# Retention with its fp32 operands kept as pairs of 16-bit parts, and small work moved between VectorE, ScalarE and GpSimd

## The chip, the cores and the metric

The kernel runs on one core of one Trainium2 chip. The metric is the device time of one execution in microseconds, and the time of a kernel is the median over its runs. Five engines work side by side, each through its own row of instructions in order: TensorE (PE; its weight loads are shown as PEld), VectorE (DVE), ScalarE (ACT), GpSimd (POOL) and SyncE (SP), which starts transfers. They wait for each other by semaphores alone.

## The reference

The program is a two-layer decoder on x of 2 x 1024 x 256 with a context of 2 x 154 x 192: a table-based attention, a cross attention and a mixture of experts in the first layer, then multi-scale retention, a headed cross attention and a signed feed-forward in the second. Every sublayer is pre-norm with a residual. The change touches retention alone, which has 16 heads with keys of 16 and values of 32:

```
x  = layernorm(x)                                  # rows of 256
q, k, v, g = x@q_w+q_b, (x@k_w+k_b)*16**-0.5, x@v_w+v_b, x@g_w+g_b
qr, kr = theta_shift(q, sin, cos), theta_shift(k, sin, cos)
mask   = where(tril, exp(diff*decay), 0);  mask /= sqrt(mask.sum(-1))
qk     = einsum('bhmd,bhnd->bhmn', qr, kr) * mask
qk     = qk / clip(abs(qk.sum(-1)), 1)
out    = einsum('bhmn,bhnd->bhmd', qk, v)
out    = (out - out.mean(-1)) / sqrt(out.var(-1) + 1e-5)    # per head, 32 wide
y      = (silu(g) * out) @ o_w + o_b               # and x += y
```

## The kernel before

All 2048 rows of x stay in SBUF as 16 tiles `x[:, t]` of 128 rows by 256. `retention` (L2608) works through the tiles in a software pipeline that is written out by hand: every engine runs `for s in STEPS` with s from -2 to 18, and in step s it works on tile s for the scores and the state, s+1 for values and turned queries and keys, s+2 for the projection and rotation of queries and keys, s-1 for the products and gates, s-2 for the gated output and s-3 for the residual. The rows of x for tile s+4 are turned and those of tile s+5 are normalised (`x_center`). The order of the calls in each loop is the order of the instructions on that engine. Nothing else orders the work but the semaphores.

Eight tiles make one batch (TB = 8). Inside a tile all 128 x 128 scores are formed; what lies in earlier tiles of the batch comes through a state `us` of (16 keys + 16 idle rows) x 33 per head, which `state` updates on VectorE from `delta`'s product and multiplies by a decay, and which is spread over four head rows into `u` for the next tile. So the first tile of each batch (t = 0 and 8) has no product with the state.

One step in the order of the data, with the lines of before:

- PE `qk` (L2948, 6 matmuls of 512 columns, 16-bit parts) projects into the bank `psq`. VectorE `rotate` turns it there in four operations (L2779, 2780, 2781, 2785), the last of which writes the fp32 tile `rot` (16 elements a head, and 16 zeros) and frees psq (`rot_done`).
- PE `turn_qk` transposes the queries, ScalarE copies them to `qkT` (L2859), then the same for the keys. Both copies are 512 wide and use the one bank `ptr`.
- PE `score` (L2922) multiplies keys and queries in fp32, two halves of 8 matmuls with K=32; each half fills `pss`. ScalarE `high` (L2852) takes a 16-bit copy of 1024 columns, VectorE `low` (L2726) the 16-bit rest, and GpSimd `mask` (L2686) zeroes the future in both parts, two operations a half.
- PE `values` (L2948) projects into the bank `psv`. ScalarE copies it twice, as 16-bit (L2867, `vhi_done`) and as fp32 `v32` (L2868, `v_done`); VectorE takes the difference of the two copies (`values_low`, L2734).
- PE `weigh` fills `pso`: for each of four groups of heads one fp32 product with the state `u` of 132 columns (L2937) and twelve 16-bit ones of 33 columns (L2941). PE `delta` (L3022) forms keys times values in fp32, 16 matmuls of 33 columns in four column groups.
- ScalarE `squares` copies pso (L2843) and squares it (L2845). VectorE `centre` has four operations: two on the row factors (L2762, L2763, 16 elements each), the sum of the squares (L2765), and the variance (L2767). GpSimd `power` raises it to -0.5 (L2705).
- PE `gates` projects the gates into the same bank `psv`; ahead of it stands a wait for v_done, since the values of tile s+1 must have left it. ScalarE `silu` (L2879), then VectorE `gate` in two operations (L2749, and L2752 after pow_done) gives `z`; it is turned, split in two 16-bit parts, multiplied by the output weights (L2982) and added to x.
- GpSimd `expand` (L2695) spreads the state into `u`, one operation of 528 elements.

Every fp32 matmul shows as two records on PE. `own.link` or `L` marks an instruction and lets the next one on the same engine wait for its end. A bank such as psv is one PSUM bank, and the trace names it `r_psv`.

Of the kernel before, what the change touches and what calls it, by code (L numbers as in the profile page):

```python
# [17 lines left out]
P = 128  # L18
# [2352 lines left out]
def tables():  # L2371
# [16 lines left out]
    floor = lay(EPS * total)  # L2388
# [5 lines left out]
class Ahead:  # L2394
# [6 lines left out]
    def __init__(self, nc, ctx, signals, x):  # L2401
# [15 lines left out]
        self.normed, self.turned = sem("normed"), sem("turned")  # L2417
# [76 lines left out]

    def turn(self, t_, t, ps):
# [36 lines left out]
    def on_vector(self, v, own, event, added, ps):  # L2532
# [50 lines left out]
    def on_scalar(self, a, event, ps):  # L2583
# [7 lines left out]
        if event == (1, 5):  # L2591
# [3 lines left out]
            a.mul(self.bhi[r, 0:D], self.brow[r], GAIN).then_inc(self.b_high, 1)  # L2595
            a.mul(self.b16[0:1, 0:D], self.brow[0:1], GAIN).then_inc(self.b_high, 1)
# [11 lines left out]
def retention(nc, x, ins, ahead, opening):  # L2608
# [3 lines left out]
    with ExitStack() as ctx:  # L2612
# [28 lines left out]
        names = ("qk_ready rot_done q_turned q_copied k_turned k_copied v_psum v_done "  # L2641
                 "g_psum silu_done scored hi_done lo_done kept_state masked vhi_done vlo_done d_ready u_done pv_done cen_done sq_done sq_used centred pow_done "
                 "z_ready z_turned zhi_done z_split o_ready x_added").split()
        (qk_ready, rot_done, q_turned, q_copied, k_turned, k_copied, v_psum, v_done,
         g_psum, silu_done, scored, hi_done, lo_done, kept_state, masked, vhi_done, vlo_done, d_ready, u_done, pv_done, cen_done, sq_done, sq_used, centred, pow_done,
# [15 lines left out]
        def _(sp):  # L2661
            for dst, nm in ((rfloor, "floor"), (keep, "keep")):
                sp.dma_start(dst[:], ins["ret_" + nm]).then_inc(s_norm, 16)
# [5 lines left out]
        def _(g):  # L2669
            own = Tally(g, s_g)  # L2670
            g.memset(rot[:, :, :, :, KD:2 * KD], 0.0).then_inc(s_c, 1)
            g.memset(v32[:, :, :, VD:VC], 1.0).then_inc(s_c, 1)
            g.memset(v16[:, :, 0, :, VD:VC], 1.0).then_inc(s_c, 1)
            g.memset(v16[:, :, 1, :, VD:VC], 0.0).then_inc(s_c, 1)
            own.link(g.memset(rowtile[:], 0.0))
            for h in range(4):
                own.link(g.memset(rowtile[32 * h:32 * h + 32, h:h + 1], 1.0))
            ahead.power(g, 2)
# [11 lines left out]
            def expand(t):  # L2690

                if inside(t) and t % TB != TB - 1:
                    g.wait_ge(kept_state, t + 1)
                    wait(g, pv_done, t)
                    g.tensor_tensor(u[:, (t + 1) % 2], us[:, t % 2].unsqueeze(2).broadcast_to((P, 4, 4, VC)),  # L2695
                                    rowtile[:].unsqueeze(1).unsqueeze(3).broadcast_to((P, 4, 4, VC)), ALU.mult).then_inc(u_done, 1)
                elif inside(t):
                    g.wait_ge(kept_state, t + 1)
                    g.tensor_copy(tiny[:], us[:, t % 2, 0, 0:1]).then_inc(u_done, 1)

            def power(t):
# [14 lines left out]
        def _(v):  # L2716
# [22 lines left out]

            def x_center(t):  # L2740
                if inside(t) and t >= FIRST:
                    ahead.center(v, t)
# [12 lines left out]
            def centre(t):  # L2755

                if inside(t):
                    q = t % 2
                    low_, var = sm[:, q, 0, :], sm[:, q, 1, :]
                    v.wait_ge(s_norm, 2 * 16)  # L2760
                    v.wait_ge(cen_done, t + 1)
                    L(v.scalar_tensor_tensor(low_, cen[:, q, :, VD], EPS, cen[:, q, :, VD], ALU.mult, ALU.mult))  # L2762
                    L(v.tensor_tensor(low_, low_, rfloor[:, t % TB, :], ALU.max))  # L2763
                    v.wait_ge(sq_done, t + 1)
                    v.tensor_reduce(var, sq[:], AX_X, ALU.add).then_inc(sq_used, 1)  # L2765
                    v.wait_ge(sq_used, t + 1)
                    v.scalar_tensor_tensor(var, var, 1.0 / VD, low_, ALU.mult, ALU.add).then_inc(centred, 1)  # L2767

            def rotate(t):
                if inside(t):  # L2770
# [7 lines left out]
                    wait(v, rot_done, t)  # L2778
# [900 lines left out]
```

## Time and profile before

| | us |
|---|---|
| median of 3 runs | 1028.42 |
| lowest and highest | 1023.22, 1030.12 |
| profiled execution, its time | 1025.94 |
| profiled execution, its span | 1024.1 |
| mean granted TensorE clock | 0.949 of full |

The profile is of one execution. Its page gives the busy time of each engine, groups of equal instructions by line, and the chain of work that ended last. A duration of a PE matmul contains the way through the array, so in a dense row the distance from start to start is the time it costs. On ScalarE and VectorE instructions that don't depend on each other overlap by about 0.09 us, which the timeline shows as a next start ahead of the end. PEclk is the granted clock as a share of 2.4 GHz; 0.50 is 1.2 GHz.

### The profile page before, as it was taken

How to read it: one execution, taken by the hardware profiler on the slowest of the kernel's cores; microseconds unless marked ns; L12 is line 12 of the kernel's file. 1: busy time of each engine (PE TensorE's matmuls, PEld its weight loads, DVE VectorE, ACT ScalarE, POOL GpSimd, SP SyncE). 2: the span in 40 equal slices, each digit the busy share in tenths (PEclk: the TensorE clock that was granted, in tenths of full speed). 3: DMA queues.
4: the chain of work that ended last, by engine and by line, in shares of the span. 5: the costliest groups of instructions: out<-in, count | busy, mean ns of one | idle time of the engine just before them, and what ended most of it. 6: DMA issues, size and time to landing. Idle time of an engine off the chain costs nothing. (4 is left out here: it accounts for less than half of the span.)

```text
span 1024.1 us, 22180 instructions
## 1 busy us (share of the span) xinstructions
PE 874.4 (85%) x8762; PEld 579.5 (57%) x8762; DVE 784.2 (77%) x1460; ACT 615.7 (60%) x1108; POOL 372.5 (36%) x326
## 2 busy tenths in 40 slices
PE   1386878788488899999689999998799998999997
PEld 0122323232246555565356777776689975778786
DVE  8899989833788899887678899887577886667443
ACT  5578789887476554452155555554578865656431
POOL 1043435321247140000246667666144641224220
PEclk9998889898679899999899999999799999999999
DMA  5403232320420030000120000000200000000000
GB/s 148 83 1 48 36 54 32 48 37 1 135 72 1 2 135 1 1 2 1 58 111 1 3 2 2 2 3 2 73 2 2 2 1 1 2 12 11 12 22 31
DMA packets 21670, 30.47 MB, mean 30 GB/s; under 512 B 6000, under 2 KB 17982, under 8 KB 20416
## 3 DMA queue, kind: packets, MB, share of 16 engines
q1 hardware_dynamic: 18816, 26.44, 11.2%
q10 hardware_dynamic: 2752, 2.62, 0.9%
q8 instruction: 70, 1.15, 0.5%
q14 instruction: 32, 0.26, 0.1%
HBM read 18.56 MB, written 2.10 MB: 20 GB/s over the span
## 5 line engine op out<-in xcount | busy, mean ns | idle before, releaser
L589 ACT ACTIVATE t_pT<-t_sc 128x1536 f32<-128x1536 f32 x96 | 136.7, 1454 | 28.8 <-PE t_sc L696 28.5
L269 POOL TENSOR_SCALAR_AFFINE_SELECT t_pT<-t_pT 128x512 f32<-128x512 f32 x64 | 75.9, 1206 | 167.4 <-ACT t_pT L589 167.3
L696 PE MATMUL t_sc<-t_qk 32*128 32x512 f16 (+3 forms) x1152 | 89.1, 365 | 47.4 <-DMA t_qk<-t_sin_parts 26.6
L696 PEld LDWEIGHTS t_sc<-t_qk 32*128 32x128 f16 x1152 | 37.1, 99 | 107.0 <-issue 50.4
L2686 POOL TENSOR_SCALAR_AFFINE_SELECT r_att<-r_att 128x1024 f16<-128x1024 f16 x64 | 69.5, 1108 | 66.2 <-DVE r_att L2726 66.2
L717 PE MATMUL t_ot<-t_pT,t_v 128*17 128x512 f32 (+3 forms) x768 | 81.3, 535 | 11.3 <-DVE t_ou L433 5.1
L1983 PE MATMUL c_pso<-ck_VO,c_pT 128*128 128x256 f16 x480 | 55.0, 273 | 1.4 <-DVE c_pT L1824 1.4
L2726 DVE TENSOR_TENSOR r_att<-r_pss,r_att 128x1024 f16<-128x1024 f32 x32 | 39.1, 1221 | 20.2 <-ACT r_att L2852 20.2
L1983 PEld LDWEIGHTS c_pso<-ck_VO,c_pT 128*128 128x128 f16 x480 | 46.3, 98 | 6.7 <-DVE c_pT L1824 1.6
L2268 ACT ACTIVATE m_sg<-m_psg 128x512 f32<-128x512 f32 x32 | 19.1, 596 | 51.6 <-PE m_psg L2311 51.5
L2852 ACT CAST r_att<-r_pss 128x1024 f16<-128x1024 f32 x32 | 32.4, 1012 | 28.0 <-PE r_pss L2922 28.0
L1894 ACT ACTIVATE c_pt<-c_pss,c_mx 128x154 f32<-128x154 f32 x128 | 48.4, 415 | 1.1 <-DVE c_mx L1807 1.1
L2332 PE MATMUL m_acc<-gw_down,m_hp 128*128 128x256 f16 x384 | 47.2, 273 | 1.9 <-DVE m_hp L2224 1.4
L2948 PE MATMUL r_psv<-ra_w,ra_xT 128*128 128x512 f16 x192 | 46.8, 380 | 1.0 <-ACT r_v L2868 1.0
L2705 POOL TENSOR_TENSOR r_sm<-r_sm,ra_sm 128x16 f32<-128x16 f32 x16 | 46.3, 2895 | 3.6 <-DVE r_sm L2767 2.0
L717 PEld LDWEIGHTS t_ot<-t_pT,t_v 128*17 128x17 f32 x768 | 17.5, 102 | 51.8 <-issue 37.6
L1774 POOL TENSOR_TENSOR c_pn<-c_pt,c_tot 128x208 f32<-128x208 f32 x16 | 24.1, 1507 | 58.3 <-DVE c_tot L1814 58.3
L2332 PEld LDWEIGHTS m_acc<-gw_down,m_hp 128*128 128x128 f16 x384 | 36.9, 98 | 12.4 <-DVE m_hp L2224 2.0
L2922 PEld LDWEIGHTS r_pss<-r_qkT 32*128 32x128 f32 x512 | 31.0, 186 | 13.6 <-issue 11.2
L2922 PE MATMUL r_pss<-r_qkT 32*128 32x128 f32 x512 | 37.1, 283 | 1.0 <-DVE r_att L2726 1.0
L2859 ACT COPY r_qkT<-r_ptr 128x512 f32<-128x512 f32 x32 | 18.8, 588 | 29.7 <-PE r_ptr L2996 29.7
L1824 DVE TENSOR_TENSOR c_pT<-c_pst,c_pT 128x512 f16<-128x512 f32 (+1 forms) x48 | 28.7, 598 | 10.3 <-ACT c_pT L1905 9.4
(593 smaller groups left out, 2408.7 us busy)
## 6 DMA issues: line engine op xcount, KB each, us to landing
t_qk<-t_cos_parts SPq DMA_DIRECT2D x24, 128.0 KB, 5.4
t_qk<-t_sin_parts SPq DMA_DIRECT2D x24, 128.0 KB, 7.0
x<-in_x ACTq DMA_DIRECT2D x4, 512.0 KB, 7.3
out_x<-x SPq DMA_DIRECT2D x8, 256.0 KB, 2.1
r_rcos<-in_ret_cos SPq DMA_DIRECT2D x1, 1280.0 KB, 9.1
r_rsin<-in_ret_sin SPq DMA_DIRECT2D x1, 1280.0 KB, 10.6
t_qk<-t_cos_parts SPq DMA_DIRECT2D x16, 64.0 KB, 2.7
gw_raw<-in_gateT SPq DMA_DIRECT2D x1, 1024.0 KB, 7.6
```

What stands on the lines that cost most here:

```text
L269: last = g.affine_select(out=blk, in_=blk, compare_op=ALU.is_ge, fill=0.0, base=0, pattern=[[0, 4], [1, P]], channel_multiplier=-1)
L589: a.activation(pT[:, at:at + 3, :].rearrange("p a s -> p (a s)"), sc[s % 2][:], ACT.Exp, scale=CURVE * CURVE / math.sqrt(2 * DH)).then_inc ...
L696: last = t.matmul(sc[s % 2][:, 512 * k + at:512 * k + at + w], qk[r, g % 3, 1, of_k, P * i:P * i + P], qk[r, g % 3, 0, of_q, q0:q0 + w], s ...
L717: last = t.matmul(ot[j][32 * h:32 * h + DH + 1, 512 - w:512], v1[:, b, 4 * c + h, i, :], pT[:, (4 * slot + h) % RING, at:at + w], start=be ...
L1894: last = a.activation(pt[:, q, h, :], pss[:, k, n * CTX:n * CTX + CTX], ACT.Exp, bias=mx[:, q, 3 * k + n:3 * k + n + 1], scale=1.0, accum_ ...
L1983: last = mm(pso[:, 0:D], l, r, start=(n == 0), stop=(n == len(todo) - 1))
L2332: last = mm(acc[:, j, :], hp[:, k, ph_, P * j:P * j + P], dw[:, pw, D * e:D * e + D], start=(e == 0 and j % 2 == 0 and ph_ + pw == 0), sto ...
L2686: last = g.affine_select(out=blk, in_=blk, compare_op=ALU.is_ge, fill=0.0, base=0, pattern=[[0, 8], [1, P]], channel_multiplier=-1)
L2705: g.tensor_tensor(sm[:, q, 2, :], sm[:, q, 1, :], ahead.sm[:, 4, 0:1].broadcast_to((P, HR)), ALU.pow).then_inc(pow_done, 1)
L2726: v.tensor_tensor(att[:, t % 2, 1, 2 * j:2 * j + 2].rearrange("p h g m -> p (h g m)"), pss[:].rearrange("p j m -> p (j m)"), att[:, t % 2, ...
L2922: last = mm(pss[:, j, P * g:P * g + P], qkT[r, q, 1, g, :], qkT[r, q, 0, g, :], start=(g == 0), stop=True, skip_group_check=True)
L2948: last = mm(d, l, r, start=(i == 0), stop=(i == len(todo) - 1))
```

## The change

- `rot`, `qkT`, `u` and the operands of `delta` are 16-bit. Each head of `rot` holds a 16-bit high part and the 16-bit rest side by side (16 + 16, in place of the zeros), and a third plane holds the keys with the two swapped. Scores are the product with the keys plus the product with the swapped keys, so each half has 16 matmuls; `delta` has 64 (keys and swapped keys, values' high and low part), and the state goes into pso by two 16-bit matmuls a group.
- `rotate` ends in psq. A new ScalarE copy `rotated_high` and a new VectorE subtraction `rotated_low` fill `rot`, and psq is free with `rot_low`. GpSimd `swap` writes the third plane in two copies.
- On ScalarE the queries' copy comes before `rotated_high`, the keys' copy is 1024 wide, and `expand` is there now as four ACTIVATEs of 264 elements with the scale from `rowtile`, between the keys' copy and the values' copy; GpSimd splits the state in two parts (`split_state`). `v32` and its copy go; `values_low` reads psv itself and stands earlier in VectorE's row.
- `x_center` moves from VectorE to the end of ScalarE's step. The row factors of `centre` (`low_`, `var`) are on GpSimd, ahead of pow, as five small operations with another table `floor`; the factor sqrt(32) that this leaves in z is taken out in `add` and in the bias row.
- PE's waits for v_done become waits for vlo_done, those for rot_done become rot_low or swapped.

```diff
@@ gpsimd
-            def expand(t):
+            def split_state(t):
                 if inside(t) and t % TB != TB - 1:
                     g.wait_ge(kept_state, t + 1)
-                    wait(g, pv_done, t)
-                    g.tensor_tensor(u[:, (t + 1) % 2], us[:, t % 2].unsqueeze(2).broadcast_to((P, 4, 4, VC)),
-                                    rowtile[:].unsqueeze(1).unsqueeze(3).broadcast_to((P, 4, 4, VC)), ALU.mult).then_inc(u_done, 1)
+                    wait(g, u_done, t)
+                    own.link(g.tensor_copy(us16[:, t % 2, 0], us[:, t % 2]))
+                    g.tensor_tensor(us16[:, t % 2, 1], us[:, t % 2], us16[:, t % 2, 0], ALU.subtract).then_inc(us_split, 1)
+            def swap(t):
+                    g.wait_ge(rot_low, t + 1)
+                    g.tensor_copy(swap_[:, :, 0:KD], keys[:, :, KD:2 * KD])
+                    g.tensor_copy(swap_[:, :, KD:2 * KD], keys[:, :, 0:KD]).then_inc(swapped, 1)
             def power(t):
-                    g.wait_ge(centred, t + 1)
+                    g.wait_ge(cen_done, t + 1)
+                    own.link(g.tensor_tensor(low_, cen[:, q, :, VD], rfloor[:, t % TB, 0, :], ALU.mult))
+                    own.link(g.tensor_tensor(low_, low_, low_, ALU.mult))
+                    own.link(g.tensor_scalar(low_, low_, 1.0, None, ALU.max))
+                    own.link(g.tensor_tensor(low_, low_, rfloor[:, t % TB, 1, :], ALU.mult))
+                    g.wait_ge(sq_used, t + 1)
+                    own.link(g.tensor_tensor(var, var, low_, ALU.add))
@@ vector
             def values_low(t):
                     v.wait_ge(vhi_done, t + 1)
-                    v.wait_ge(v_done, t + 1)
-                    v.tensor_tensor(v16[:, q, 1, :, 0:VD], v32[:, q, :, 0:VD], v16[:, q, 0, :, 0:VD], ALU.subtract).then_inc(vlo_done, 1)
+                    v.scalar_tensor_tensor(v16[:, q, 1, :, 0:VD], psv[:].rearrange("p (h d) -> p h d", h=HR), 1.0 / GAIN,
+                                           v16[:, q, 0, :, 0:VD], ALU.mult, ALU.subtract).then_inc(vlo_done, 1)
+            def rotated_low(t):
+                    v.wait_ge(rot_high, t + 1)
+                    v.tensor_tensor(parts[:, :, :, KD:2 * KD], psq[:].rearrange("p (a h d) -> p a h d", a=2, h=HR),
+                                    parts[:, :, :, 0:KD], ALU.subtract).then_inc(rot_low, 1)
@@ scalar
+            def rotated_high(t):
+                    a.wait_ge(rot_done, t + 1)
+                    a.copy(rot[:, t % ROTS, 0:2, :, 0:KD], psq[:].rearrange("p (a h d) -> p a h d", a=2, h=HR)).then_inc(rot_high, 1)
+            def expand(t):
+                    a.wait_ge(us_split, t + 1)
+                    wait(a, pv_done, t)
+                    for h in range(4):
+                        last = a.activation(u[:, (t + 1) % 2, :, :, h, :], us16[:, t % 2], ACT.Copy, scale=rowtile[:, h:h + 1])
+                    last.then_inc(u_done, 1)
             for s in STEPS:
                 high(s, 0)
                 squares(s - 1)
                 high(s, 1)
                 copy_turned(s + 1, 0, q_turned, q_copied)
+                rotated_high(s + 2)
                 copy_turned(s + 1, 1, k_turned, k_copied)
+                expand(s - 1)
                 values(s + 1)
                 z_high(s - 2)
                 x_high(s + 4)
                 silu(s - 1)
+                x_center(s + 5)
@@ tensor
-                            last = mm(pss[:, j, P * g:P * g + P], qkT[r, q, 1, g, :], qkT[r, q, 0, g, :], start=(g == 0), stop=True, skip_group_check=True)
+                            mm(pss[:, j, P * g:P * g + P], qkT[r, q, 1, g, :], qkT[r, q, 0, g, :], start=(g == 0), stop=False, skip_group_check=True)
+                        for j in range(2):
+                            h = 2 * half + j
+                            r = slice(32 * h, 32 * h + 32)
+                            last = mm(pss[:, j, P * g:P * g + P], qkT[r, q, 2, g, :], qkT[r, q, 0, g, :], start=False, stop=True, skip_group_check=True)
             def gates(t):
-                    upto(t_, v_done, t + 3)
+                    upto(t_, vlo_done, t + 3)
                     wait(t_, z_ready, t)
                     project(t, psv[:], 1024, g_psum)
```

ScalarE's row of one full step before, from the second score half (`high(s, 1)`) to the next one; `r_v` are the values, `ra_xT` the turned rows of x:

```order
L2852 CAST r_att<-r_pss 128x1024
L2859 COPY r_qkT<-r_ptr 128x512 x2
L2867 ACTIVATE r_v<-r_psv 128x16x32
L2868 ACTIVATE r_v<-r_psv 128x16x32
L2874 CAST r_zT<-r_ptr 128x512
L2506 CAST ra_xT<-r_psq 128x2x128
L2879 ACTIVATE r_psv<-r_psv 128x512
L2852 CAST r_att<-r_pss 128x1024
```

And the same stretch in the change:

```order
L2882 CAST r_att<-r_pss 128x1024
L2890 COPY r_qkT<-r_ptr 128x512
L2897 CAST r_rot<-r_psq 128x32x16
L2890 COPY r_qkT<-r_ptr 128x1024
L2907 ACTIVATE r_u<-r_us,r_rowtile 128x8x33 x4
L2916 ACTIVATE r_v<-r_psv 128x16x32
L2922 CAST r_zT<-r_ptr 128x512
L2519 CAST ra_xT<-r_psq 128x2x128
L2927 ACTIVATE r_psv<-r_psv 128x512
L2505 ACTIVATE ra_xn<-x,ra_sm 128x255
L2882 CAST r_att<-r_pss 128x1024
```

Six instructions more stand in a step and one less; five of them are ahead of the values' copy (`r_v`), and the last, x_center, is ahead of the next scores' copy.

GpSimd's row of a step in the change, from its four masks to the next ones; before, L2705 and L2695 stood in place of all that is between them (L2736 is the new line of pow, `r_us` the state):

```order
L2701 AFFINE_SELECT r_att<-r_att 128x1024 x4
L2721 COPY r_rot<-r_rot 128x16x16
L2722 COPY r_rot<-r_rot 128x16x16
L2730 TENSOR_TENSOR r_sm<-r_cen,r_rfloor 128x16
L2731 TENSOR_TENSOR r_sm<-r_sm 128x16
L2732 TENSOR_SCALAR r_sm<-r_sm 128x16
L2733 TENSOR_TENSOR r_sm<-r_sm,r_rfloor 128x16
L2735 TENSOR_TENSOR r_sm<-r_sm 128x16
L2736 TENSOR_TENSOR r_sm<-r_sm,ra_sm 128x16
L2710 CAST r_us<-r_us 128x132
L2711 TENSOR_TENSOR r_us<-r_us 128x132
L2701 AFFINE_SELECT r_att<-r_att 128x1024 x4
```

Seven small operations are now ahead of pow in its row, and two behind it.

## Rows read from the trace of the kernel before

**Rows 1.** The page, part 1: busy us (share of the span) x instructions.

```profile
PE 874.4 (85%) x8762; PEld 579.5 (57%) x8762; DVE 784.2 (77%) x1460; ACT 615.7 (60%) x1108; POOL 372.5 (36%) x326
```

**Rows 2.** Windows: stretch, its length, busy us of each engine, PEclk, DMA share, GB/s.

```profile
600.00:700.00 100.00, 99.39 (x1368) 72.89 (x1369) 86.14 (x162) 53.73 (x88) 69.14 (x52) 1.00 0.01 2
```

**Rows 3.** Waits of 520 to 705 us: who waited for whom, total, times, longest.

```profile
POOL r_att L2686 <- DVE r_att L2726: 66.2, 31, 10.2
ACT r_att L2852 <- PE r_pss L2922: 28.0, 29, 2.5
...
PEld r_psv L2948 <- ACT r_v L2868: 4.2, 14, 0.7
```

**Rows 4.** Timeline of one step: start, us, engine, line, operation, shapes, count, [idle before].

```profile
599.81 0.49 PE L2937 MATMUL r_pso<-r_u,r_qkT 128*128 128x132 f32 x2
...
599.98 1.01 ACT L2852 CAST r_att<-r_pss 128x1024 f16<-128x1024 f32 x1 [0.57 <-PE r_pss L2922]
...
600.14 0.46 PE L2941 MATMUL r_pso<-r_v,r_att 128*128 128x33 f16 x12
...
600.45 0.47 PE L2937 MATMUL r_pso<-r_u,r_qkT 128*128 128x132 f32 x2
...
601.03 1.23 DVE L2726 TENSOR_TENSOR r_att<-r_pss,r_att 128x1024 f16<-128x1024 f32 x1 [1.29 <-ACT r_att L2852]
...
602.49 0.69 DVE L2749 TENSOR_TENSOR r_psv<-r_psv,r_cen 128x512 f32<-128x512 f32 x1
...
603.21 0.69 DVE L2752 TENSOR_TENSOR r_z<-r_psv,r_sm 128x512 f32<-128x512 f32 x1
...
603.82 0.41 DVE L2779 TENSOR_TENSOR r_rb<-r_psq,r_rsin 128x256 f32<-128x256 f32 x1
...
605.26 1.47 PE L2982 MATMUL r_psd<-ra_wo,r_zT 128*128 128x256 f16 x12
605.34 0.69 DVE L2785 TENSOR_TENSOR r_rot<-r_psq,r_rb 128x512 f32<-128x512 f32 x1
...
608.51 0.46 PE L3022 MATMUL r_psd<-r_v,r_rot 128*32 128x33 f32 x32
...
609.75 0.98 PEld L2948 LDWEIGHTS r_psv<-ra_w,ra_xT 128*128 128x128 f16 x6 [0.22 <-ACT r_v L2868]
...
611.15 1.16 PE L2922 MATMUL r_pss<-r_qkT 32*128 32x128 f32 x16
611.26 0.58 ACT L2879 ACTIVATE r_psv<-r_psv 128x512 f32<-128x512 f32 x1 [0.81 <-PE r_psv L2948]
...
612.24 0.49 PE L2937 MATMUL r_pso<-r_u,r_qkT 128*128 128x132 f32 x2
```

**Rows 5.** Timeline in the table attention: 16-bit matmuls with K=32.

```profile
153.41 0.83 PE L696 MATMUL t_sc<-t_qk 32*128 32x512 f16 x12 [0.53 <-ACT t_pT L589]
```

**Rows 6.** Timeline: four ACTIVATEs, scale and bias from a tile.

```profile
340.02 2.10 ACT L846 ACTIVATE ce_room<-x,mr_sm 128x256 f16<-128x256 f32 x4
```

**Rows 7.** ScalarE's groups by form: line, operation, shapes, count, busy us, mean ns.

```profile
L1537 ACT ACTIVATE c_A<-c_pso,c_a_gain 128x308 f16<-128x308 f32 x1 | 0.5, 517 | 1.0 <-PE c_pso L1581 1.0
L1541 ACT ACTIVATE c_row_high<-c_extra 1x308 f16<-1x308 f32 x1 | 0.4, 417 | 1.0 <-PE c_extra L1697 1.0
...
L2859 ACT COPY r_qkT<-r_ptr 128x512 f32<-128x512 f32 x32 | 18.8, 588 | 29.7 <-PE r_ptr L2996 29.7
```

**Rows 8.** GpSimd's groups by form, the same columns.

```profile
L2705 POOL TENSOR_TENSOR r_sm<-r_sm,ra_sm 128x16 f32<-128x16 f32 x16 | 46.3, 2895 | 3.6 <-DVE r_sm L2767 2.0
...
L2695 POOL TENSOR_TENSOR r_u<-r_us,r_rowtile 128x528 f32<-128x528 f32 x14 | 15.1, 1077 | 0.0
...
L2699 POOL COPY r_tiny<-r_us 128x1 f32<-128x1 f32 x2 | 0.4, 184 | 0.0
```

**Rows 9.** Windows at the end of retention, the columns of rows 2.

```profile
712.50:715.00 2.50, 0.80 (x6) 0.42 (x4) 2.04 (x4) 0.46 (x2) 0.44 (x1) 1.00 0.00 0
715.00:716.50 1.50, 0.14 (x1) 0.13 (x2) 0.69 (x1) 0.58 (x1) 0.00 (x0) 0.55 0.00 0
```

More of the change, by code:

```diff
@@ L2493, in center, with offsets, center_on_scalar @@
                         ALU.subtract, ALU.mult).then_inc(self.normed, 1)
+    def offsets(self, v, n):
+        t = slice(*self.SPANS[n])
+        v.wait_ge(self.rs_ready, n + 1)
+        v.scalar_tensor_tensor(self.sm[:, 0, t], self.sm[:, 1, t], -1.0, self.sm[:, 3, t], ALU.mult, ALU.mult).then_inc(self.nm_ready, 1)
+    def center_on_scalar(self, a, t):
+        a.wait_ge(self.nm_ready, sum(t >= b for b, _ in self.SPANS[1:]))
+        wait(a, self.turned, t - 1)
+        a.activation(self.xn[:, t % 2, 0:D - 1], self.x[:, t, 0:D - 1], ACT.Identity, bias=self.sm[:, 0, t:t + 1],
+                     scale=self.sm[:, 3, t:t + 1]).then_inc(self.normed, 1)
     def turn(self, t_, t, ps):
@@ L2709, in _ @@
                 mask(s, 1)
+                swap(s + 2)
                 power(s - 1)
-                expand(s)
+                split_state(s)
                 if s in (8, 14):
@@ L2817, in _ @@
                 low(s, 1)
+                rotated_low(s + 2)
                 centre(s - 1)
+                values_low(s + 1)
                 state(s)
@@ L2821, in _ @@
                 z_low(s - 2)
-                values_low(s + 1)
                 x_low(s + 4)
@@ L2883, in x_high, with x_center @@
                     ahead.high(a, t, psq)
+            def x_center(t):
+                if inside(t) and t >= FIRST:
+                    ahead.center_on_scalar(a, t)
             for s in STEPS:
@@ L2961, in values @@
                     wait(t_, z_ready, t - 2)
-                    wait(t_, v_done, t)
+                    wait(t_, vlo_done, t)
                     project(t, psv[:], 512, v_psum)
@@ L3016, in delta @@
                     q = t % 2
-                    t_.wait_ge(v_done, t + 1)
-                    t_.wait_ge(rot_done, t + 1)
+                    t_.wait_ge(vlo_done, t + 1)
+                    t_.wait_ge(swapped, t + 1)
                     wait(t_, kept_state, t)
                     for g in range(4):
-                        for h in range(4):
-                            last = mm(psd[32 * h:32 * h + 32, VC * g:VC * g + VC], rot[:, t % ROTS, 1, 4 * g + h, :], v32[:, q, 4 * g + h, :],
-                                      start=(g == 0), stop=True, skip_group_check=True)
+                        for which, part in itertools.product((1, 2), range(2)):
+                            for h in range(4):
+                                last = mm(psd[32 * h:32 * h + 32, VC * g:VC * g + VC], rot[:, t % ROTS, which, 4 * g + h, :], v16[:, q, part, 4 * g + h, :],
+                                          start=(g == 0 and which == 1 and part == 0), stop=(which == 2 and part == 1), skip_group_check=True)
                     last.then_inc(d_ready, 1)
```

115 lines of the change are left out of this document (62 added, 53 removed).

## The prediction

> **What bounds the kernel now.** I read the page first, then the time windows, then the waits of the retention stage, and last one step of it on the timeline. The page gives PE 85% of the span, DVE 77%, ACT 60%, POOL 36% [rows 1]. The change touches one stage, retention, from 506 to 720 us on the timeline; its few small edits outside keep the same instructions. In the window 600 to 700 PE is busy for 99.4 us of 100, DVE for 86, POOL for 69 and ACT for 54, at the full clock [rows 2]. The waits agree: POOL waits for DVE 66.2 us and ACT for PE 28.0, while the largest wait of PE's side for another engine in these 185 us is 4.2 us, a weight load held back by ScalarE's copies of the values [rows 3]. So PE sets the length of a step. The reader sees that length by taking the first `r_pso<-r_u` matmul of two steps: 599.81 and 612.24, so 12.43 us [rows 4].
>
> PE fills these 12.43 us without a gap. Its parts that the change touches, by start to start: a score half 1.09 (611.15 to 612.24), and two of them in a step; a weigh group 0.31 for one fp32 matmul on the state and 0.31 for twelve small ones (599.81, 600.14, 600.45), four groups in a step; delta, 32 records in 0.46 with the last one's end [rows 4].
>
> **What the change takes from PE.** Per step:
> - Scores: 8 fp32 matmuls (16 records, 1.09 us) become 16 16-bit ones of the same 128 columns. The trace has no K=32, 128-column 16-bit row inside retention, but twelve of 512 columns over four row groups take 0.83 us with the last one's end [rows 5], under 70 ns each, where L2982's 109 ns for 256 columns make it 218 for one alone: three run beside each other. Two row groups instead of four and a quarter of the columns give some 30 ns, so 16 are 0.5 us; without overlap 55 ns each, 0.85. I take 0.55: 0.54 less, twice, 1.1 us.
> - Weigh: four fp32 132-column matmuls of 0.31 become eight 16-bit ones. By the 256-column row (12 in 1.47 us less 0.16 for the last one's end, 109 ns [rows 4]) 132 columns are some 55 ns: 0.44 for 1.24, 0.8 less, in the 14 of 16 tiles that have a state.
> - Turns: 8 fp32 transposes become 12 16-bit ones of some 55 ns each. The fp32 ones can't be under that; at twice it they were 0.9, and 0.2 goes (bounds 0 and 0.25).
> - Delta: 32 records in 0.4 become 64: 0.8 at the same rate, 0.4 if each costs half. I take 0.7: 0.3 more.
> Together 12.43 - 1.1 - 0.8 - 0.2 + 0.3 = 10.6 us of PE work in a step (10.2 to 11.5). If PE stayed the bound the stage would lose 1.8 us a step.
>
> **What is late next.** I follow what PE will wait for. `gates(s-1)` writes psv, so it must wait until `values` of tile s+1 have left psv. Before, two ScalarE copies did that (v_done), and PE waited 0.22 us for it [rows 4]. Now `values_low` on VectorE reads psv too, so PE waits for vlo_done; and on ScalarE the copy `vhi` now stands behind `rotated_high`, a copy twice as wide and four expansions. That closes a loop through four engines. One turn of it, each term by start to start from the rows of before, hand-over included:
> - gates on PE to silu on ACT: 609.75 to 611.26, 1.51 [rows 4]
> - silu, 0.58 less the 0.09 by which the next one overlaps it, 0.49; then x_center, which now stands ahead of the next `high`: four of 256 columns with scale and bias from a tile take 2.10 us, 0.50 apart [rows 6]. The next score half needs 1.40 + 0.55 + 0.11 = 2.06 us from the start of gates, less than 1.51 + 0.49 + 0.50 = 2.50, so it is hidden and x_center is not.
> - high(s,0) to low(s,0): 1.05 (599.98 to 601.03); low 1.23 less 0.09, 1.14; gate 0.72 + 0.61 [rows 4]
> - rotate: three operations 1.52 (603.82 to 605.34), and the fourth with its hand-over 0.69 + 0.05 [rows 4]
> - new on ACT: rotated_high like L2859, 0.59 less 0.09, 0.50; the keys' copy of 1024 columns like L2852's 1.01, 0.91 [rows 4, 7]
> - new on ACT: expand, four ACTIVATEs of 264 columns whose scale is read from a tile. L1537 is the same operation on 308 columns from PSUM, 517 ns, where a constant scale takes 417 (L1541) [rows 7]. 44 columns less, at 0.82 ns (588 to 1012 ns from 512 to 1024), is 481, less 0.09 for the overlap: 0.39. From the other side, the four of rows 6, from SBUF and with two operands from a tile, come 0.50 apart. I take 0.45, between them; four are 1.80.
> - vhi 0.60 (512 columns, as L2859) and 0.04 to DVE; values_low 0.69 and 0.06 to PE
> The sum is 1.51 + 0.99 + 1.05 + 1.14 + 1.33 + 1.52 + 0.74 + 0.50 + 0.91 + 1.80 + 0.64 + 0.75 = 12.88 us. With 0.05 for a hand-over the loop is 12.9, against 12.43 before. Its ends are 12.6 (expand 0.39 each) and 13.2 (0.50 each and 0.1 more for the wide 16-bit copy).
>
> Before, the loop didn't exist: ScalarE came to the values' copies as soon as PE had projected them. ScalarE's busy share grows only from 54% to some 70%, so what costs is where the work stands in its row, not how much there is.
>
> The Trainium skill, in "ScalarE: Activation LUTs", section "What ACT_TABLE_LOAD costs", says that a pointer operand adds about 93 ns and that back-to-back ACTIVATEs overlap by about as much. The rows L1537 and L1541 agree (100 ns). By its formula expand would be an estimated 0.41 each, and the step 12.7.
>
> **What is off the loop.** VectorE loses x_center and three of centre's four operations and gains one of 512 columns (rotated_low, 0.69), so its work shrinks, and that only lengthens its waits. GpSimd gains swap (two copies of 256, priced by L2695, two operands and 528 columns in 1.08: 0.4 to 0.7 each), five 16-element operations at 0.2 to 0.25 each (one element takes 0.18, L2699) and two of 132 in place of L2695 [rows 8]: 69 us of 100 become some 80. What it adds waits as follows: gate waits for pow_done, and queued behind gate on DVE is rotate and the whole step. From low(s,1)'s end: two masks 2.25, swap 1.0, small operations 1.25, pow 2.9, so 7.4; then gate's second half 0.61, rotate 1.52 + 0.61 and low(s+1,1) 1.22, 4.0: 11.4, 1.5 us short of the bound. Covered.
> On SP one small table doubles; the step that waits for it is some 10 us behind its issue.
>
> **The sum over the stage.**
> - Eight of the fifteen steps have all parts and lie where PE was the bound: 12.9 - 12.43, 0.46 each; one more, where PE was not yet full, 0.6: +4.3.
> - The step where the second batch begins: weigh has no state there, PE was 1.2 us shorter and the loop isn't: +1.7.
> - The first two +0.1; the last three have no x_center, so the loop is 12.4, as PE was: +0.3.
> - The start: rotated_high and rotated_low stand ahead of the second tile's projection (0.64 + 0.69), and the keys' copy of tile 0 waits behind rotated_high of tile 1 (0.5) and is 0.4 longer: +2.3.
> - The tail after the last scores: fp32 matmuls gone, two score halves (1.1) and the turns: -1.2.
> Together +7.5 us. The profiled execution took 1025.9 us for a span of 1024.1; the median of the runs shown is 1028.4, 2.5 above it.
> To this comes the clock. PE will stand still 12.9 - 10.6 = 2.3 us in every step, at one place, ahead of gates, with delta and fp32 transposes just ahead of it. The trace has such a pause: between 712.5 and 715.0 PE was busy 0.80 of 2.50 us, and in the next 1.5 us the granted clock was 0.55, nearly the lower level of 0.50 (1.2 GHz) [rows 9]. Against it: the pause here is one, with 10.6 us of work between two. Where it falls over gates, its 6 matmuls take 1.4 us more, and they are in the loop. I count two of the thirteen steps, +3.
> Forecast: 1025.9 + 7.5 + 3 = 1036.4 in the profile's terms, 1038.9 against the median: 1% slower.
>
> **Rivals.**
> 1. PE stays the bound, or the loop is much cheaper (the change does what it takes from PE). For it: everything above has PE at 99%. Against it: the loop's terms are measured ones but for expand. It would need 1.5 us less, as with expand at 0.2 each and x_center and the keys' copy 0.25 shorter each. Then GpSimd's 11.4 is next: -1.0 x 13 - 1 = -14, 1014.
> 2. The loop, without any fall of the clock, with expand between 0.39 and 0.45: +4 to +7.5, so 1030 to 1033.5, and 1032 to 1036 against the median. Within 1%.
> 3. The clock falls in most steps: 7 x 1.4 and a little for scores and weigh, +11 on the loop's +7.5: 1047; with a longer expand 1052. The Trainium skill ("TensorE: Matmul & The Clock Gate", "What's actually happening") calls the throttled state the default one that activity lifts, which speaks for this. It decides from the point where PE's pause stays near 2.3; if scores and delta cost 0.85 and 1.2, the pause is 1.2 and no such fall is seen in the trace.
> 4. GpSimd's row is longer: if swap and its small operations come to over 3.8 us instead of 2.2, pow_done passes 12.9. At 4.5, +0.75 x 12: 1045. For it: pow itself takes 2.9 for 16 elements [rows 8]. Against it: 0.18 for the one-element copy.
> Chances: forecast with a few falls 0.34, rival 2 0.30, rival 3 0.17, rival 4 0.07, rival 1 0.12. One per cent (10 us) is about what a measurement of this kernel can tell from no change. The forecast's own cases lie on the edge of it, two thirds over. With two thirds of the forecast, all of rivals 3 and 4 and none of rival 2, slower by over 1% has 0.46, within 0.42, faster 0.12. The range leaves out most of rival 1 and the top of rival 3: 1020 to 1054.
>
> **What would show it.** Right: a step of 12.7 to 13.3 us; PE busy 80 to 85% in retention; one PE wait per step before the gates' matmuls, released by VectorE's values_low, of about 2 us; VectorE idle before values_low, released by ScalarE; expand near 0.54 us each. The score halves at half their time or less confirm the part on PE. Wrong: no PE wait ahead of gates, a step under 12.2, or GpSimd without idle time before its masks. If the granted clock in retention is 1.0 throughout, the 3 us go; under 0.9, rival 3.

## The result, and the profile after

| | before | changed kernel |
|---|---|---|
| median of 5 runs | 1028.42 us (1023.11 to 1030.12) | 1037.77 us (1036.34 to 1043.5) |
| ratio, 95% interval | | 1.0115 [1.0071, 1.016] |
| profiled execution, its span | 1025.94, 1024.1 us | 1037.56, 1035.8 us |

The change costs 1.15%: the ratio is of the means of the runs (1038.6 and 1026.8), where the two medians alone would give 0.9%. The forecast was 1038.9. One execution of the kernel before beside the later variants took 1920.92 us and is left out of the ratios.

The page of the changed kernel, part 1, answers to [rows 1]:

```profile
PE 852.0 (82%) x9338; PEld 553.0 (53%) x9338; DVE 767.9 (74%) x1418; ACT 651.8 (63%) x1184; POOL 391.7 (38%) x452
```

PE, DVE and PEld have less to do, ACT and POOL more, and the span is longer: no engine was pushed to its limit, so the time is in waits. The windows of the changed kernel, the columns of [rows 2, 9]:

```profile
600.00:700.00 100.00, 83.48 (x1507) 55.45 (x1505) 73.88 (x139) 67.18 (x121) 76.27 (x112) 0.95 0.01 2
...
562.00:564.00 2.00, 0.50 (x3) 0.27 (x4) 1.22 (x4) 1.46 (x4) 1.75 (x7) 1.00 0.00 0
564.00:566.00 2.00, 2.00 (x11) 0.63 (x11) 1.57 (x4) 0.18 (x1) 1.84 (x3) 0.50 0.00 0
566.00:568.00 2.00, 2.00 (x51) 1.80 (x47) 0.11 (x1) 1.86 (x3) 1.92 (x3) 0.65 0.03 8
```

PE was busy for 99.4 us of 100 and is now at 83.5. The three short windows show what [rows 9] showed once before: PE stands still (busy 0.50 of 2.00), and then its granted clock is 0.50, the lower level of 1.2 GHz, for some three microseconds. Such a stretch is called a fall below.

The waits of 520 to 705 us in the changed kernel, as in [rows 3]:

```profile
POOL r_att L2701 <- DVE r_att L2758: 41.2, 21, 3.6
PEld r_psv L3008 <- DVE r_v L2765: 27.5, 13, 2.2
...
ACT r_psv L2927 <- PE r_psv L3008: 24.5, 13, 2.8
PE r_psv L3008 <- DVE r_v L2765: 24.4, 13, 2.0
DVE r_v L2765 <- ACT r_v L2916: 23.9, 16, 2.5
```

Read the last three as parts of a ring. PE's gates wait for VectorE's `values_low` (L2765), 13 times about 1.9 us. `values_low` waits for ScalarE's values' copy (L2916). ScalarE's silu (L2927) waits for the gates. The rest of the ring is the order of ScalarE's and VectorE's own rows. Before, PE's largest wait here was 4.2 us in all.

The timeline of one step of it, as in [rows 4], with the operations of that loop, the start of a score half, delta and pow:

```profile
599.50 1.74 ACT L2907 ACTIVATE r_u<-r_us,r_rowtile 128x264 f16<-128x264 f16 x4
...
601.13 0.59 ACT L2916 ACTIVATE r_v<-r_psv 128x512 f16<-128x512 f32 x1
...
601.75 0.69 DVE L2765 SCALAR_TENSOR_TENSOR r_v<-r_psv,r_v 128x512 f16<-128x512 f32 x1 [1.44 <-ACT r_v L2916]
...
602.50 1.47 PE L3008 MATMUL r_psv<-ra_w,ra_xT 128*128 128x512 f16 x6 [1.95 <-DVE r_v L2765]
...
603.51 2.93 POOL L2736 TENSOR_TENSOR r_sm<-r_sm,ra_sm 128x16 f32<-128x16 f32 x1
...
603.90 0.23 PE L2977 MATMUL r_pss<-r_qkT 32*128 32x128 f16 x2
...
604.01 0.58 ACT L2927 ACTIVATE r_psv<-r_psv 128x512 f32<-128x512 f32 x1 [1.54 <-PE r_psv L3008]
...
604.46 0.29 PE L2997 MATMUL r_pso<-r_u,r_qkT 128*128 128x132 f16 x2
604.50 0.59 ACT L2505 ACTIVATE ra_xn<-x,ra_sm 128x255 f32<-128x255 f32 x1
...
604.99 1.00 ACT L2882 CAST r_att<-r_pss 128x1024 f16<-128x1024 f32 x1
...
606.03 1.22 DVE L2758 TENSOR_TENSOR r_att<-r_pss,r_att 128x1024 f16<-128x1024 f32 x1 [1.46 <-ACT r_att L2882]
...
607.17 0.69 DVE L2777 TENSOR_TENSOR r_psv<-r_psv,r_cen 128x512 f32<-128x512 f32 x1
...
607.89 0.69 DVE L2780 TENSOR_TENSOR r_z<-r_psv,r_sm 128x512 f32<-128x512 f32 x1
...
608.50 0.41 DVE L2801 TENSOR_TENSOR r_rb<-r_psq,r_rsin 128x256 f32<-128x256 f32 x1
...
610.01 0.70 DVE L2804 TENSOR_TENSOR r_psq<-r_psq,r_rb 128x512 f32<-128x512 f32 x1
...
610.82 0.58 ACT L2897 CAST r_rot<-r_psq 128x512 f16<-128x512 f32 x1 [1.13 <-DVE r_psq L2804]
611.30 1.02 ACT L2890 COPY r_qkT<-r_ptr 128x1024 f16<-128x1024 f16 x1
611.59 0.66 PE L3086 MATMUL r_psd<-r_v,r_rot 128*32 128x33 f16 x64
...
612.21 0.54 ACT L2907 ACTIVATE r_u<-r_us,r_rowtile 128x264 f16<-128x264 f16 x1
```

Leave out GpSimd's pow (L2736) and PE's scores, state product and delta (L2977, L2997, L3086), which are not in the loop, and follow the other starts from top to bottom: each operation starts as the one before it ends, on the same engine or, after a wait, on another. `expand` (L2907) comes round after 612.21 - 599.50 = 12.71 us; its last line shows only the first of its four operations, since the view ends there. Between 535 and 665 us ten steps lie: seven take 12.71 or 12.72, and three 13.57, 14.05 and 13.55. The three are those in which the clock falls.

### The profile page after: what moved, and what is told of

It is laid out like the page before. It is cut to its first block and busy times, and to the rows that moved or that the text cites. A ratio compares the mean times of both kernels' runs of the same rounds, so it can differ in the third digit from the quotient of the medians.

```text
span 1035.8 us, 23523 instructions
## 1 busy us (share of the span) xinstructions
PE 852.0 (82%) x9338; PEld 553.0 (53%) x9338; DVE 767.9 (74%) x1418; ACT 651.8 (63%) x1184; POOL 391.7 (38%) x452
## 5 line engine op out<-in xcount | busy, mean ns | idle before, releaser
L269 POOL TENSOR_SCALAR_AFFINE_SELECT t_pT<-t_pT 128x512 f32<-128x512 f32 x64 | 73.3, 1166 | 168.4 <-ACT t_pT L589 168.4
L696 PE MATMUL t_sc<-t_qk 32*128 32x512 f16 (+3 forms) x1152 | 86.6, 357 | 48.8 <-DMA t_qk<-t_sin_parts 26.2
L2701 POOL TENSOR_SCALAR_AFFINE_SELECT r_att<-r_att 128x1024 f16<-128x1024 f16 x64 | 68.5, 1094 | 42.4 <-DVE r_att L2758 41.7
L3008 PE MATMUL r_psv<-ra_w,ra_xT 128*128 128x512 f16 x192 | 52.4, 414 | 25.9 <-DVE r_v L2765 25.9
L2736 POOL TENSOR_TENSOR r_sm<-r_sm,ra_sm 128x16 f32<-128x16 f32 x16 | 46.8, 2926 | 1.2
L3008 PEld LDWEIGHTS r_psv<-ra_w,ra_xT 128*128 128x128 f16 x192 | 17.9, 102 | 46.5 <-DVE r_v L2765 29.2
L2882 ACT CAST r_att<-r_pss 128x1024 f16<-128x1024 f32 x32 | 32.3, 1009 | 12.8 <-PE r_pss L2981 12.7
L1905 ACT CAST c_pT<-c_pst 128x512 f16<-128x512 f32 (+1 forms) x48 | 25.2, 528 | 17.9 <-PE c_pst L1973 17.9
L2311 PE MATMUL m_psg<-m_xT,gw_gate 128*128 128x512 f16 x144 | 35.0, 379 | 0.0
```

The lines of the kernel that those rows point to most:

```text
L269: last = g.affine_select(out=blk, in_=blk, compare_op=ALU.is_ge, fill=0.0, base=0, pattern=[[0, 4], [1, P]], channel_multiplier=-1)
L696: last = t.matmul(sc[s % 2][:, 512 * k + at:512 * k + at + w], qk[r, g % 3, 1, of_k, P * i:P * i + P], qk[r, g % 3, 0, of_q, q0:q0 + w], s ...
L2701: last = g.affine_select(out=blk, in_=blk, compare_op=ALU.is_ge, fill=0.0, base=0, pattern=[[0, 8], [1, P]], channel_multiplier=-1)
L2736: g.tensor_tensor(sm[:, q, 2, :], var, ahead.sm[:, 4, 0:1].broadcast_to((P, HR)), ALU.pow).then_inc(pow_done, 1)
L3008: last = mm(d, l, r, start=(i == 0), stop=(i == len(todo) - 1))
```

## The experiments

All are edits of the changed kernel. Times are medians; the ratios are to the kernel before, run beside each on the same chip (medians of before 1026.3 beside e1, e2, e3 and e5, 1027.3 beside e4, e6, e7 and e8, 1026.0 beside e9 and e10).

| run | edit | us | ratio, 95% interval | full step | clock 524.5 to 700 |
|---|---|---|---|---|---|
| changed kernel | | 1037.77 | 1.0115 [1.0071, 1.016] | 12.71 | 0.96 |
| e1 | expand behind the values' copy | 1018.1 | 0.9926 [0.9899, 0.9953] | 11.48 | 1.00 |
| e2 | x_center ahead of silu | 1036.0 | 1.0088 [1.006, 1.0116] | 12.35 | 0.96 |
| e3 | matmuls in PE's pause | 1032.35 | 1.006 [1.0038, 1.0083] | 12.71 | 1.00 |
| e5 | two more copies on GpSimd | 1041.73 | 1.0155 [1.0133, 1.0177] | 12.72 | 0.94 |
| e8 | e5 and e3 | 1032.96 | 1.0056 [1.0038, 1.0074] | 12.71 | 1.00 |
| e4 | x_center back on VectorE | 1043.01 | 1.0152 [1.012, 1.0183] | 12.81 | 0.93 |
| e7 | e1 and e3 | 1024.58 | 0.9971 [0.9952, 0.9991] | 11.89 | 1.00 |
| e6 | e1, x_center at the end of VectorE's step | 1018.05 | 0.9905 [0.9876, 0.9933] | 11.40 | 1.00 |
| e9 | e6, swap behind the powers | 1013.68 | 0.9875 [0.9851, 0.9899] | 11.11 | 1.00 |
| e10 | e1, swap behind the powers | 1017.54 | 0.9913 [0.9892, 0.9934] | 11.48 | 1.00 |

### Is it the place of expand in ScalarE's row?

```diff
                 copy_turned(s + 1, 1, k_turned, k_copied)
-                expand(s - 1)
                 values(s + 1)
                 z_high(s - 2)
                 x_high(s + 4)
+                expand(s - 1)
                 silu(s - 1)
```

> ScalarE's four expansions moved from ahead of the values' copy to just ahead of silu, where ScalarE stood idle 1.5 us per step in the changed kernel (silu waited 26.3 us for PE over the stage); nothing else is changed. Theory (the loop gates, silu, x_center, high, low, gate, rotate, rotated_high, keys' copy, expand, vhi, values_low sets the step): the 1.63 us of expand leave the loop, silu then waits for expand a little instead, so a step goes from 12.71 to about 11.4 us, PE's wait ahead of gates from 1.95 to about 0.6 us, the clock no longer falls in the stage (3 us), and the kernel takes 1018 to 1024 us, under the kernel before. Rival (ScalarE's amount of work or another chain sets the step): the same work in another place changes nothing, 1035 to 1039.

1018.1 us. Nothing is taken away, the same 23 thousand instructions run, and the kernel goes from slower than before to faster. Timeline of one step of e1:

```profile
602.10 0.62 ACT L2916 ACTIVATE r_v<-r_psv 128x512 f16<-128x512 f32 x1
...
602.31 0.63 PE L3068 MATMUL r_ptr<-ra_ident,r_z 128*128 128x128 f32 x4 [0.33 <-issue]
...
602.97 0.59 ACT L2922 CAST r_zT<-r_ptr 128x512 f16<-128x512 f32 x1 [0.26 <-PE r_ptr L3068]
...
603.57 1.47 PE L3008 MATMUL r_psv<-ra_w,ra_xT 128*128 128x512 f16 x6 [0.42 <-DVE r_v L2765]
603.72 1.74 ACT L2907 ACTIVATE r_u<-r_us,r_rowtile 128x264 f16<-128x264 f16 x4
...
605.35 0.59 ACT L2927 ACTIVATE r_psv<-r_psv 128x512 f32<-128x512 f32 x1
...
606.19 2.93 POOL L2736 TENSOR_TENSOR r_sm<-r_sm,ra_sm 128x16 f32<-128x16 f32 x1
...
606.36 1.00 ACT L2882 CAST r_att<-r_pss 128x1024 f16<-128x1024 f32 x1
...
609.32 0.69 DVE L2780 TENSOR_TENSOR r_z<-r_psv,r_sm 128x512 f32<-128x512 f32 x1
```

`expand` now runs while PE computes the gates for which ScalarE had waited 1.54 us anyway. PE's pause shrinks from 1.95 to 0.42 us, the step from 12.71 to 11.48, and the clock stays at 1.00. `silu` starts right at the end of `expand`, 1.78 us after the gates where the changed kernel has 1.51, so `expand` still holds it up by 0.27 us. What sets the start of `expand` is now ScalarE's copy of the turned z (L2922), which waits 0.26 us for PE's turn (L3068). In the profiles the stage, from its first projection to the first matmul of the cross attention, takes 226.25 us in the changed kernel, 208.33 in e1 and 215.25 before.

### Is x_center in the loop?

```diff
                 x_high(s + 4)
+                x_center(s + 5)
                 silu(s - 1)
-                x_center(s + 5)
```

> x_center on ScalarE moved from behind silu to just ahead of it, where ScalarE waits for PE's gates; nothing else. Theory: 0.44 us a step leave the loop (0.50 less what the score half then needs), in some 10 steps: 12.71 goes to 12.3, the kernel to 1031 to 1035. Rival (x_center is hidden behind the score half, and only expand and the keys' copy count): 1036 to 1039.

The normal step shrinks to 12.35, by 0.36: x_center was in the loop, and before `silu` it lies in a wait. It is 0.36 and not 0.44, since the next `high` now starts 2.12 us after the gates (616.29 to 618.41), where 2.06 had been reckoned. The time, 1036.0, lies outside what was expected, at the rival's edge, and it is the step that decides against the rival: the stage is 1.3 us shorter in the profile, where ten steps of 0.36 would be 3.6. The clock's falls took back the rest. They make steps of 13.45, 13.97 and 13.94: 1.1, 1.6 and 1.6 over the normal one, where those of the changed kernel are 0.9, 1.3 and 0.8 over. One more, 12.70 among the last steps, is 1.4 over e3's 11.31, where the changed kernel's is 0.95 over.

### What do the falls cost?

The matmuls below compute nothing that is used: they write spare columns of pso and fill PE's pause.

```diff
                 turn_x(s + 4)
+                if inside(s) and inside(s - 1):
+                    t_.wait_ge(sq_done, s)
+                    t_.wait_ge(cen_done, s)
+                    for i in range(24):
+                        mm(pso[:, 1, 264:388], one16[:], xT[:, i % 4, 0:124], start=False, stop=True, skip_group_check=True)
                 gates(s - 1)
```

> 24 matmuls of 124 columns more on PE in each step, into columns of the product bank that nobody reads, just ahead of gates' wait: some 1.3 us of PE work inside the pause of about 2 us. It computes nothing. Theory (PE is no bound, and three falls of the granted clock cost 3.0 us): the fillers are free and keep the clock up, so granted clock 0.99 to 1.00 from 525 to 700 us against 0.96, and 1033 to 1036 us. Rival A (PE still bounds): plus 1.3 us in 15 steps, 1053 to 1058. Rival B (fillers are free but the falls of the clock cost nothing or don't hang on the pause): 1037 to 1039 with the clock at 0.96.

Windows of e3:

```profile
524.50:700.00 175.50, 161.59 (x3161) 114.84 (x3157) 130.53 (x236) 123.54 (x218) 135.17 (x198) 1.00 0.01 3
```

The clock is 1.00 and all full steps take 12.71 (one 12.78). Extra work for PE makes the kernel faster than the changed one: 1.006 of before for 1.0115, some 5 us. The two intervals still touch (1.0083 and 1.0071), so the size rests on the traces. By them the falls cost 3.0 us in the full steps (0.86 + 1.27 + 0.84, the middle one against e3's 12.78), 0.95 in one of the last steps (12.26 for 11.31 in e3) and 0.85 in the tail (from the last `expand` but one to cross attention 20.82 for 19.97 us): 4.8 us. The whole stage takes 221.52 us in e3, 4.7 less than in the changed kernel. The time is a little under the 1033 to 1036 that was expected. Of the 17.9 us that e1 takes from the stage, 13.2 are left beside e3, where no fall is either.

### Is GpSimd hidden?

The two copies write a spare tile that nobody reads.

```diff
                     g.tensor_copy(swap_[:, :, 0:KD], keys[:, :, KD:2 * KD])
+                    own.link(g.tensor_copy(spare[:], keys[:, :, KD:2 * KD]))
+                    own.link(g.tensor_copy(spare[:], keys[:, :, 0:KD]))
                     g.tensor_copy(swap_[:, :, KD:2 * KD], keys[:, :, 0:KD]).then_inc(swapped, 1)
```

> GpSimd's swap copies twice as much: two more copies of 256 elements into a tile that nobody reads, 0.8 to 0.9 us more a step ahead of its small operations and pow. Theory (GpSimd is covered: it waited 2.4 us for VectorE ahead of its second masks): pow_done comes 0.9 later and still within the step, 1037 to 1040. Rival (GpSimd's row is the bound or level with it): 0.85 us in 14 steps, 1048 to 1051.

1041.73 lies above what was expected, though its interval overlaps that of the changed kernel. The step between falls stays at 12.72, but there are six longer ones before 706 us where the changed kernel has four. Either the falls are all of it, or the copies cost something else. e8 has the copies of e5 and the matmuls of e3:

> e5 (two more copies on GpSimd) with e3's fillers, so that the granted clock stays up. Theory (e5's step between falls is 12.71 as in the change, and its 4 us over it are falls of the clock in other places): with the clock at 1.0 the copies cost nothing and the time is e3's, 1030 to 1034. Rival (the copies cost by themselves): e3 plus 3 to 11, 1036 to 1043.

1.0056 beside 1.006 of e3, and a stage of 221.48 us beside 221.52: at a steady clock the copies cost nothing. GpSimd is hidden in the changed kernel, and what e5 cost was the clock.

### x_center where it had been

```diff
-                if s == STEPS[0]:
-                    ahead.offsets(v, 1)
-                if s == STEPS[0] + 3:
-                    ahead.offsets(v, 2)
+                x_center(s + 5)
                 gate(s - 2)
@@ scalar
-                x_center(s + 5)
```

> The change with x_center back on VectorE where it was, between low and gate; expand stays ahead of the values' copy. Theory: what x_center took from the loop on ScalarE (0.36, as e2 showed) it gives back on VectorE, where it stands in the same loop (0.31): a step of 12.6 to 12.7, 1035 to 1038. Rival (moving work off ScalarE helps by its length): 12.2, 1030 to 1033.

This missed. The normal step is 12.81 and not under 12.7, as x_center takes its turn on VectorE inside the same loop, and it holds the loop up there for 0.47 us (from 612.25 to gate's start at 612.72), where 0.31 had been reckoned. And seven of twelve steps are long, 13.2 to 14.4 us; the clock is 0.93. So the change's move of x_center to ScalarE was no loss, but a small gain of 0.1 us a step. Of the falls this run says only that more of them came at a slightly longer step; why so many more is open.

### What bounds it once expand is late?

e7 adds the matmuls of e3 to e1:

> The kernel of e1 with the 24 filler matmuls of e3 (1.3 us of PE a step that compute nothing). Theory: the loop of e1 leaves PE only 0.4 to 0.9 us ahead of gates, so here PE becomes the bound: plus 0.4 to 0.9 a step, 1024 to 1031 us, where the same fillers cost e3 nothing. Rival (PE's work doesn't count in any of these orders): 1017 to 1020.

PE is busy for 168.55 of 175.50 us (e1: 156.19) and the step is 11.89, 0.41 longer than e1's. There is no clock to win back, PE has 0.4 us of pause a step, and the fillers exceed it. Beside e3's unchanged step of 12.71 this says that the fillers help by the clock alone.

e6 takes x_center off ScalarE in e1 and puts it at the end of VectorE's step, for tile s + 6:

> The kernel of e1 (expand ahead of silu, 11.48 us a step) with x_center taken off ScalarE again and put at the end of VectorE's step, where VectorE waits 0.66 us for ScalarE. Theory: x_center's 0.50 us between silu and the next score copy are in the loop of e1 too; without them the copy starts when the scores are there, so 0.2 to 0.5 less a step, 11.0 to 11.3, and 1012 to 1016 us. Rival (in e1 PE or GpSimd sets the step already): 1017 to 1020.

Missed as well: 11.40 us a step and not 11.0 to 11.3, and 1018.05 us and not 1012 to 1016. Its timeline shows what took over:

```profile
601.82 1.21 DVE L2758 TENSOR_TENSOR r_att<-r_pss,r_att 128x1024 f16<-128x1024 f32 x1
...
603.10 2.14 POOL L2701 TENSOR_SCALAR_AFFINE_SELECT r_att<-r_att 128x1024 f16<-128x1024 f16 x2 [1.24 <-DVE r_att L2758]
...
605.18 0.46 POOL L2721 COPY r_rot<-r_rot 128x256 f16<-128x256 f16 x1
...
607.49 2.93 POOL L2736 TENSOR_TENSOR r_sm<-r_sm,ra_sm 128x16 f32<-128x16 f32 x1
...
610.51 0.69 DVE L2784 TENSOR_TENSOR r_z<-r_psv,r_sm 128x512 f32<-128x512 f32 x1 [0.34 <-DVE r_psv L2781]
...
613.24 1.22 DVE L2758 TENSOR_TENSOR r_att<-r_pss,r_att 128x1024 f16<-128x1024 f32 x1
```

`low` of the second half frees the masks (L2701), then come swap (L2721), the small operations and pow (L2736). Pow ends at 610.42, and 0.09 later gate's second half (L2784) starts, which had waited 0.34 us. After it come rotate and the next `low`, 11.42 us after the first. This is the GpSimd loop that the prediction put at 11.4. The wait's label names VectorE's own product L2781; its end at 610.17 is not what released L2784, pow's is. In e1 that gate (L2780, 609.32) had started 0.20 us after pow's end at 609.12; 0.09 of it is the hand-over, so only 0.1 us a step was to be had, and 0.08 came. Swap is needed only a step later, so it can go out of this loop:

```diff
                 mask(s, 0)
                 mask(s, 1)
-                swap(s + 2)
                 power(s - 1)
+                swap(s + 2)
```

> e6_late_and_center_dve with GpSimd's order changed: the swap copies stand behind the powers instead of ahead of them. Theory: in e6 a second loop sets the step of 11.40 us, the one by way of GpSimd: low of the second half (601.82), masks, swap, five small operations, pow (ends 610.42), gate's second half (610.51), rotate, low of the next (613.24). The two swap copies take 0.77 us of it, and they are needed only a step later. Without them in front the powers end 0.77 us earlier, until gate's first half sets the start of the second: that leaves 0.34 us of idle time in e6, so the step becomes 11.05 (10.9 to 11.2), some 14 x 0.35 = 5 us less: 1012 to 1015 beside a kernel before of 1026 to 1027. Rival: GpSimd is in no loop of e6 (the scores' path over PE, ScalarE and VectorE sets the step): step 11.40, 1017 to 1019.

> e1_expand_late with the same move on GpSimd: swap behind the powers. Theory: in e1 gate's second half starts at the end of its first (609.29 and 609.32), 0.2 us after pow has ended (609.12), so GpSimd's loop is just hidden behind ScalarE's row (expand, silu, x_center, high). The move changes nothing: step 11.4 to 11.5, 1017 to 1019. Rival: GpSimd's loop sets the step in e1 as in e6: then 0.3 us a step less, 1013 to 1015.

Both came out as the theory has it: 11.11 us a step and 1013.68 in e9, 11.48 and 1017.54 in e10. In e10 the full steps stay, and the two steps near the end that have no x_center shrink from 11.16 and 11.42 to 10.84 and 10.87. In the timeline of e9 gate's halves are back to back and no longer wait for pow, which ends at 609.16:

```profile
602.57 2.13 POOL L2701 TENSOR_SCALAR_AFFINE_SELECT r_att<-r_att 128x1024 f16<-128x1024 f16 x2 [1.10 <-DVE r_att L2758]
...
606.24 2.92 POOL L2736 TENSOR_TENSOR r_sm<-r_sm,ra_sm 128x16 f32<-128x16 f32 x1
...
609.06 0.69 DVE L2781 TENSOR_TENSOR r_psv<-r_psv,r_cen 128x512 f32<-128x512 f32 x1
...
609.78 0.69 DVE L2784 TENSOR_TENSOR r_z<-r_psv,r_sm 128x512 f32<-128x512 f32 x1
```

e9 is the best version: 1.25% faster than before, and 0.9875 / 1.0115 = 0.976 of the changed kernel, by three operations put elsewhere. What sets its 11.11 was not tested; in its trace VectorE's `low` waits 0.21 us for ScalarE's `high`, ahead of which silu and `expand` run without a pause.

## Why the prediction was right

Both its steps held: a loop through PE, ScalarE and VectorE takes PE's place as the bound, and the pause that it leaves costs clock. (The prediction speaks of four engines; its own terms name three, and GpSimd is off this loop, as e8 shows.)

**PE's work.** A score half was priced at 0.55 and takes 0.56 (603.90 to 604.46); delta 0.7 and 0.66. Of a step of 12.71 PE stands still 1.95, so its work and short gaps are 10.76; 10.6 was said, with a pause of 2.3.

**The loop.** 12.9 was said, 12.71 came. By start to start on the timeline: gates to silu 1.51 (said 1.51), silu 0.49 (0.49), x_center 0.49 (0.50), high to low 1.04 (1.05), low 1.14 (1.14), gate 1.33 (1.33), rotate 1.51 + 0.81 (1.52 + 0.74), rotated_high 0.48 (0.50), keys' copy 0.91 (0.91), expand 1.63 (1.80), vhi 0.62 (0.64), values_low 0.75 (0.75). The one term that was off is `expand`, and it is nearly all of the difference: 0.41 apart and not 0.45. The estimate by the Trainium skill's formula ("ScalarE: Activation LUTs", "What ACT_TABLE_LOAD costs"), 0.41 each and a step of 12.7, was the better one: this trace agrees with it.

**The stage**, in us, by the starts of VectorE's `low` in both traces:

| term | said | measured |
|---|---|---|
| entry into the stage | 0 | -0.3 |
| start, to the first `low` | +2.3 | +2.9 |
| first two steps | +0.1 | -0.1 |
| full steps, falls taken out | +4.3 | +2.6 |
| start of the second batch | +1.7 | +1.4 |
| last steps, fall taken out | +0.3 | -0.1 |
| tail, clock taken out | -1.2 | -0.5 |
| clock | +3 | +4.8 |
| behind the stage | 0 | +1.0 |
| sum | +10.5 | +11.7 |

The sum hides errors of both signs. The full steps were over-priced by 1.7. Nine were counted, and one of them, said at 0.46, had no x_center any more and took 12.34; it stands among the last steps here. The other eight were over-priced by 1.2: 0.19 a step, nearly all of it expand's 0.04 taken four times, less 0.3 because three steps of before were 12.25, 12.28 and 12.36 where one short one had been reckoned with. The tail was under-priced by 0.7: its PE work did shrink, but PE is busy for only 1.60 and 1.02 us of its last two stretches of three (727 to 733); it ends in a chain through the last gates and turns, and a quicker matmul shortens such a chain little. Before's own tail had a fall ([rows 9]: 0.55 from 715.0 us on), which the -0.5 contains, so the tail's work shrank by less still. The clock was under-counted: beside the three falls in full steps (two were said, at 1.4 each; they cost 0.8 to 1.3) there was one among the last steps and one in the tail, of which the prediction said nothing. The last 1.0 lies in stages that the change does not touch and was not traced further; the same stretch takes 302.4 to 304.0 us in the ten variants.

So the loop was reasoned, and the nearness of the sum is in part luck: the count of falls was a guess, and e5, with the same step, has six where the changed kernel has four. The 2.5 us that were added to get from the profile to the median belong to the first runs of before; its later medians lie 1.1 to 2.5 us lower.

**The rivals.** Rival 2, the loop without falls, is what e3 shows: 1.006, within 1%, with a stage 6.3 us longer than before's (+4 to +7.5 was said). It was the true alternative, and the falls decide between it and the forecast. Rival 3 (most steps) did not come in the changed kernel but came in e4. Rival 4 fell: swap and its small operations take 603.51 - 601.27 = 2.24 us, as priced, though by two errors that cancel (swap 0.71 for 1.0, the five small operations 1.53 for 1.25), and pow ends at 606.44, 1.45 us ahead of its reader at 607.89, for the 1.5 that was said. Rival 1 had its floor right: take expand and x_center out of ScalarE's way and GpSimd's 11.4 is next, which e6 and e9 confirm.

What the prediction did not see is how cheap the cure was. It priced `expand` at 1.80 us in the loop and did not ask where ScalarE would then idle: 1.54 us for the gates, three copies behind it.

## What to carry to other kernels

When work moves to an engine that is only 54% busy, ask where in that engine's row it stands: walk the ring of waits and place it in a wait that is there anyway, behind the instruction that others wait for. One line moved turned +1.15% into -0.74%. Then look for the loop that is next, since its slack (0.1 us a step in e1) caps what the following edit can give, and move out of it what has no reader there.

## What was not expected of the hardware

- A pause of PE of some 2 us, nearly the same in each step, is followed by a fall of the granted clock to 0.50 in some steps and in others is not: four of the changed kernel's, six of e5's and seven of e4's, at steps that differ by 0.1 us or nothing. Small changes elsewhere move the count, and so times by several us; what picks the steps is open. With the pause down to 0.65 us by fillers (e3, e8) or to 0.42 (e1) none came.
- 64 matmuls of 33 columns over four column groups (delta) take 0.66 us with the last one's end, some 10 ns each. Sixteen of 128 columns over two row groups take 0.56, 35 ns each, where one alone lasts 0.22.
- Four back-to-back ACTIVATEs of 264 16-bit columns with the scale from a tile take 1.74 us, 0.41 apart.
